# Reordering the beginning, the small pieces and the hand-over of an attention, gated attention and routing kernel

## The reference, cut to what matters

```python
# 1. token attention: convolutions of 3 taps, 8 heads of 16
q, k, v = (elu(conv3(x, W) + b) for W, b in ((WQ, BQ), (WK, BK), (WV, BV)))   # 8 x 748 x 128
h = softmax(q @ k.T / sqrt(16)) @ v
# 2. gated attention on layernorm(h): one more layernorm, expand, gelu gate, causal softmax
#    with a position bias, project; added to h
# 3. routed feed-forward on layernorm(h): top 2 of 64 experts with shared weights, capacity 128,
#    gelu(x w1 + b1) w2 + b2, weighed by the router; added to h
```

## Time and profile before

| | us |
|---|---|
| median of 3 runs (lowest, highest) | 840.41 (840.29, 840.66) |
| the profiled execution | 839.29 |
| its span, first to last instruction | 837.5 |
| TensorE busy | 785.9 (94%) |
| VectorE busy | 680.9 (81%) |
| ScalarE busy | 511.1 (61%) |
| POOL busy | 270.5 (32%) |

### The profile page before, as it was taken

The page is one execution under the profiler, slowest core; times in us unless marked ns, Lnnn a source line. Parts: engine busy times, 40 slices in busy tenths (PEclk is TensorE's granted clock), DMA queues, the critical chain, the costliest instruction groups (busy, mean ns, idle before and its releaser), DMA issues. The chain is left out here.

```text
span 837.5 us, 15609 instructions
## 1 busy us (share of the span) xinstructions
PE 785.9 (94%) x5555; PEld 472.6 (56%) x5555; DVE 680.9 (81%) x1624; ACT 511.1 (61%) x1096; POOL 270.5 (32%) x281
## 2 busy tenths in 40 slices
PE   9699999999999999999999997758999999999997
PEld 5254554554554554554453432236698787887885
DVE  4898888899899899889889896437888787887866
ACT  4176776786786786786786766414646546456343
POOL 3572250252252251251352022413152333332312
PEclk9999999999999999999999999868999999999999
DMA  5370151161151162142133103000000000000001
GB/s 115 67 120 14 11 118 25 12 119 25 11 110 35 11 106 38 11 104 40 11 89 36 12 2 65 7 9 1 1 1 20 19 2 19 20 2 20 18 3 37
DMA packets 85676, 31.08 MB, mean 37 GB/s; under 512 B 58496, under 2 KB 84320, under 8 KB 85600
## 3 DMA queue, kind: packets, MB, share of 16 engines
q1 hardware_dynamic: 85360, 29.80, 19.7%
q10 hardware_dynamic: 240, 0.30, 0.2%
HBM read 4.76 MB, written 3.06 MB: 9 GB/s over the span
## 5 line engine op out<-in xcount | busy, mean ns | idle before, releaser
L446 ACT ACTIVATE probs<-ps_a 128x384 f32<-128x384 f32 (+1 forms) x732 | 304.3, 482 | 93.9 <-PE ps_a L640 85.3
L531 DVE TENSOR_REDUCE neg_max<-ps_a 128x1 f32<-128x512 f32 (+1 forms) x384 | 251.7, 679 | 42.1 <-PE ps_a L656 40.6
L640 PE MATMUL ps_a<-q_rep,k_rep 98*128 98x384 bf16 (+3 forms) x768 | 217.0, 326 | 4.5 <-DVE neg_max L533 1.6
L656 PE MATMUL ps_a<-k_rep,q_rep 96*128 96x512 bf16 (+3 forms) x768 | 202.9, 322 | 8.2 <-DVE neg_max L531 4.1
L671 PE MATMUL ps_pv<-probs,v_hat 128*32 128x364 f32 (+3 forms) x1536 | 141.9, 487 | 0.0
L640 PEld LDWEIGHTS ps_a<-q_rep,k_rep 98*128 98x128 bf16 (+1 forms) x768 | 77.9, 102 | 101.1 <-issue 37.8
L533 DVE TENSOR_REDUCE neg_max<-ps_a 128x2 f32<-128x472 f32 x192 | 122.2, 636 | 0.0
L656 PEld LDWEIGHTS ps_a<-k_rep,q_rep 96*128 96x128 bf16 (+1 forms) x768 | 77.6, 105 | 72.4 <-DVE neg_max L531 21.0
L671 PEld LDWEIGHTS ps_pv<-probs,v_hat 128*32 128x32 f32 (+1 forms) x1536 | 40.3, 109 | 55.2 <-issue 37.7
L296 POOL TENSOR_TENSOR out_n<-out_r,inv_sum 128x192 f32<-128x192 f32 x32 | 16.4, 513 | 116.3 <-DVE inv_sum L512 110.6
L270 POOL TENSOR_SCALAR qk_e<-qk_e 128x748 f32<-128x748 f32 x14 | 38.0, 2716 | 38.5 <-ACT qk_e L363 38.5
(11 more groups left out here) (225 smaller groups left out, 1171.4 us busy)
## 6 DMA issues: line engine op xcount, KB each, us to landing
q_rep<-parts_q SPq DMA_DIRECT2D x96, 96.0 KB, 3.7
k_rep<-parts_k SPq DMA_DIRECT2D x93, 96.0 KB, 3.8
hall<-out_n SPq DMA_DIRECT2D x256, 12.0 KB, 1.8
xT<-in_x SPq DMA_DIRECT2D x8, 375.0 KB, 4.1
out_h<-y_out SPq DMA_DIRECT2D x7, 320.0 KB
q_rep<-max_T SPq DMA_DIRECT2D x32, 6.0 KB
w_sb<-in_w_T SPq DMA_DIRECT2D x2, 256.0 KB, 3.5
out_h<-y_out SPq DMA_DIRECT2D x8, 54.0 KB
```

What stands on the lines that cost most here:

```text
L446: act.activation(probs[0:rows(kt), n % RING, 0:w], ps_a[0:rows(kt), 3 + n % 3, 0:w], ACT.Exp, scale=DH ** -0.5).then_inc(p_ready, 1)
L531: dve.tensor_reduce(neg_max[0:rows(t), 0, col:col + 1], ps_a[0:rows(t), c, :], AX.X, ALU.max, negate=True).then_inc(sc_max, 1)
L640: pe.matmul(out[0:rows(kt), 0:QW[qh]], k_rep[0:KM, cb % 2, h, kt * P:kt * P + rows(kt)], q_rep[0:KM, cb % 2, qh, h, 0:QW[qh]], start=True, ...
L656: last = pe.matmul(out, q_rep[0:KS, it % 2, t // QT, h, t % QT * P:t % QT * P + rows(t)], k_rep[0:KS, it % 2, h, 512:L] if c == 2 else k_r ...
```

## The change

- **Hand-over.** `spread(B - 1, 1)`, the last 16 DMAs of SP in the first block, goes to SP's program of the second block, behind the rows of unit 0's maxima there. `out_n` and its semaphore live longer for it. The statistics and scales of unit 7 go from iteration 0 to iteration 2 of the second block. `load` goes from the end of SP's unit 7 to its beginning, between the rows of the fourth quarter of unit 6 and `spread(6, 0)`.
- **Beginning.** The four pieces are now keys 0, keys 1, queries 0, queries 1, split at column 384 instead of 374, so that the first product needs only three pieces. w_k is loaded by ScalarE's queue, x first by SP. SP issues all twelve copies (six of keys, then six of queries); ScalarE issues none. The 2-row memset of `k_rep` goes ahead of POOL's other work.
- **Unit 0's small pieces.** The two copies of unit 1's keys go from VectorE to ScalarE (`first_copy_k`). `elu_v` goes from steps 2 and 4 to 9 and 10, `elu_qk` from (4, 0) and (10, 0) to (9, 2) and (11, 1), and on ScalarE `high_part` and `middle_part` of the queries go to (9, 3) and (11, 1), of the keys to (12, 1) and (14, 0).
- **Places in all other units** move by a fraction of a step or one step. POOL's order in a unit was: negative q, residue q, outputs of quarter 2, third part q, negative k, residue k, outputs of quarter 3, third part k, negative v0, negative v1. It becomes: negative q, outputs of quarter 2, residue q, negative k, third part q, outputs of quarter 3, residue k, negative v0, third part k, negative v1.

```diff
@@ SP, beginning
+        load_x(0)
+        sp.dma_start(b_col["k"][:, :], bk.rearrange("(c o) -> c o", o=1)).then_inc(loaded["k"], 16)
         load_w("q", wq)
-        load_x(0)
...
+        for t, j in sorted(enumerate(K_PART), key=lambda tj: tj[1]):
+            sp.wait_ge((p_hi, p_mid, p_split)[j], 2)
+            replicate_k(sp, 0, 0, t)
         for t, j in sorted(enumerate(Q_PART), key=lambda tj: tj[1]):
-            sp.wait_ge((p_hi, p_mid, p_split)[j], 2)
+            sp.wait_ge((p_hi, p_mid, p_split)[j], 3)
             replicate_q(sp, 0, 0, t)
...
@@ SP, units
                 maxima_rows(it - 1, 3)
-                spread(it - 1, 0)
+            if it == B - 1:
+                ahead["load"](sp)
+            if it > 0:
+                spread(sp, it - 1, 0)
...
-            if it == B - 1:
-                ahead["load"](sp)
         maxima_rows(B - 1, 3)
-        for g in range(NG):
-            spread(B - 1, g)
+        spread(sp, B - 1, 0)
@@ ScalarE, after_exp
-                if at == (2, 1):
+                if at == (2, 0):
                     exp_qk(n, "q")
-                if at == (4, 2):
+                if at == ((6, 0) if it > 0 else (9, 3)):
                     high_part(n, "q")
+                if it == 0 and at in ((3, 0), (5, 3)):
+                    first_copy_k(s // 5)
-                if at == (7, 3):
+                if at == (7, 0):
                     exp_qk(n, "k")
-                if at == (7, 3):
+                if at == ((8, 1) if it > 0 else (11, 1)):
                     middle_part(n, "q")
-                if at == (10, 0):
+                if at == ((10, 0) if it > 0 else (12, 1)):
                     high_part(n, "k")
-                if at == (12, 0):
+                if at == ((12, 0) if it > 0 else (14, 0)):
                     middle_part(n, "k")
@@ VectorE, between
-                if at in ((3, 1), (6, 0)):
+                if it > 0 and at in ((3, 1), (6, 1)):
                     copy_qk(n, 2 + (s - 3) // 3)
-                if at == (4, 0):
+                if it > 0 and at == (4, 1):
                     elu_qk(n, "q")
-                if at == (10, 0):
+                if it > 0 and at == (9, 1):
                     elu_qk(n, "k")
-                if at in ((18, 2), (22, 1)):
-                    elu_v(n, ((18, 2), (22, 1)).index(at))
+                if at in ((19, 0), (21, 0)):
+                    elu_v(n, ((19, 0), (21, 0)).index(at))
-            if at in ((6, 0), (12, 0), (18, 2)):
+            if at in ((6, 1), (12, 0), (18, 1)):
                 maxima(it, s // 6 - 1)
-            if at in ((17, 0), (23, 1), (5, 2), (11, 1)):
+            if at in ((17, 0), (23, 0), (4, 2), (11, 0)):
...
+            if it == 0 and at in ((9, 0), (10, 0)):
+                elu_v(0, s - 9)
+            if it == 0 and at in ((9, 2), (11, 1)):
+                elu_qk(n, "qk"[(s - 9) // 2])
@@ second block
+            if it == 0:
+                spread(sp, B - 1, 1)
-            if it == 0:
+            if it == 2:
                 G["scales"](pool, B - 1, plain_wait)
-            if it == 0:
+            if it == 2:
                 for done in spread_done:
-                    dve.wait_ge(done, 16 * GH * (P // 32) * B)
+                    dve.wait_ge(done, SPREAD * B)
                 G["statistics"](dve, B - 1, plain_wait)
```

More of the change, by code:

```diff
@@ L50, in plain_wait, with token_attention @@
     eng.wait_ge(sem, value)
-def token_attention(nc, ctx, hall, spread_done, ahead, x, wq, wk, wv, bq, bk, bv):
+def token_attention(nc, ctx, outputs_of, ahead, x, wq, wk, wv, bq, bk, bv):
+    hall, out_n, o_done, spread_done, spread = outputs_of
     def sb(name, shape, dt):
@@ L304, in _ @@
             n = it + 1
[L305 to L308 removed]
+            if n < B:
+                negative(n, "q")
+            if it == 0:
+                negative(n, "k")
+            else:
+                weigh_outputs(it - 1, 2)
+            if n < B:
+                residue(n, "q")
                 if it > 0:
[L310 to L312 removed]
+                    negative(n, "k")
+                third_part(n, "q")
+            if it > 0:
+                weigh_outputs(it - 1, 3)
             if n < B:
+                residue(n, "k")
+                negative(n, "v0")
+                third_part(n, "k")
                 if it == 0:
                     ones_rows(1)
[L316 removed]
                 negative(n, "v1")
@@ L1113, with gated_units @@
 AT = places()
-def gated_units(nc, ctx, G, hall, spread_done, out):
+def gated_units(nc, ctx, G, outputs_of, out):
+    hall, _, _, spread_done, spread = outputs_of
     def sb(name, shape, dt):
```

133 lines of the change are left out of this document (67 added, 66 removed).

## The result

| | before | after |
|---|---|---|
| median of 4 runs (lowest, highest), us | 840.35 (840.12, 840.66) | 833.25 (831.16, 834.34) |
| the profiled execution, us | 839.29 | 834.34 |
| its span, us | 837.55 | 832.61 |
| mean granted TensorE clock | 0.981 | 0.984 |

The ratio is 0.9912, 95% interval 0.9891 to 0.9934: faster by 0.9%. The forecast was 822.0 us with a range of 814 to 829. It was 11 us too low; the time lies above the range.

What follows compares the result with a forecast made beforehand. TensorE bounds a middle unit, VectorE unit 0's first steps. Terms -10.3 - 6.2 + 0.5 - 1.3 + 0.4 + 1.3 - 2.8 = -18.4 took 839.29 to 820.9, or 822.0 us at the median's level; range 814 to 829.

Steps and rivals of the forecast that it cites:

- The hand-over and the load: Change of blocks: sixteen DMA issues leaving SP's end gain 10.3 us, loading the second block's weights earlier gains 6.2.
- the load's +0.5: End of the first block: the load, now in front of spread(6, 0), costs 0.5 us, ends 0 and 2.5.
- its forecast case: Likeliest case, 822.0 us, chance 0.53: in unit 0, tile 24 waits 4.3 us for rows behind SP's twelve copies.
- the last starts at 19.4. It lands 3.5 us later: Beginning: SP's last of twelve copies lands so that the first product runs at about 23.1 instead of 24.26, -1.2 us.
- 0, if a landing of 4.1 and a crowded queue eat it: Beginning: the bound at which the -1.2 us term gains nothing; the other end was -2.8.
- Tile 24 waits from 55.7 to 60.0: Unit 0: TensorE, ready at 55.7, stands until quarter 1's rows arrive behind the copies of unit 1's queries.
- a new stall of 4.3: Unit 0: the cost in us of TensorE's wait at tile 24, set against 2.4 gained by beginning and pieces.
- +0.3 at quarter 0, behind a copy and a reduction: Every unit but unit 0: quarter 0's maxima come later, costing 0.3 us within a net -0.4 a unit, -2.8 in seven.
- Twelve small VectorE operations ... +0.4: Second block, iteration 2: unit 7's statistics, 1.8 us of VectorE, delay TensorE by 0.4 us, range 0 to 1.
- The clock's term: Start of the second block: a shorter pause leaves less time at half clock, -1.3 us, ends 0 and -3.
- one pause of this size only: Clock at the new block: the trace before has only one TensorE pause like that of 3.28 us, followed by half clock.
- the places cost: Rival for the units: ScalarE standing at the keys' middle part costs TensorE 0.5 us each, +3.5 for -2.8, 828.3 us; chance 0.12.

Runs made afterwards that it cites:

- e5: Changed kernel with ScalarE issuing the three copies of the keys' high part and SP the other nine: 834.82 us, ratio to the kernel before 0.9951.
- e13: Changed kernel with rows early in unit 0, quarter 0's maxima ahead, scales in iteration 3, and first queries' copies halved before the first product: 813.11 us.
- e14: Changed kernel with unit 0's queries' ELU, high, middle and third parts back at their old steps: 824.54 us, ratio to the kernel before 0.9815.
- e12: Changed kernel with 24 idle TensorE products in the stall at tile 24 of unit 0: 830.94 us, ratio to the kernel before 0.9907.
- e16: Changed kernel with ScalarE's high part of the queries at (5, 2) instead of (6, 0) in units 1 to 6: 824.18 us.
- e3: Changed kernel with the keys' second-half copy and quarter 0's maxima back ahead of reduction (6, 0) in units 1 to 7: 824.88 us.
- e4: Changed kernel with POOL computing unit 7's scales in iteration 3 of the second block instead of iteration 2: 831.98 us.
- e10: Kernel before with spread(7, 1) in the second block and unit 7's statistics and scales in iteration 2, load left in place: 828.91 us.
- e2: Changed kernel with SP sending quarter 1's rows ahead of the twelve copies of unit 1's queries in unit 0: 827.66 us.
- e15: Changed kernel with the edits of e14, e3 and e4 together: 813.83 us, ratio to the kernel before 0.9698.
- e7: Kernel before with the hand-over edits, new places in units 1 to 7 (quarter 0's maxima as in e3) and e4's scales; old beginning and unit 0: 815.44 us.
- e11: Kernel before with only the load of the second block's weights moved ahead of spread(6, 0): 834.07 us, ratio 0.9953.
- e9: Changed kernel with rows early in unit 0, e3's and e4's edits, and twelve idle TensorE products ahead of the first score product: 816.58 us.

## Why the prediction was wrong

**Right.** The hand-over and the load, term by term (10.8 for 10.3, 6.7 for 6.2), and that they add up, the load's +0.5 apart; `repeat_weights` behind the maxima; the second block's start. Right in kind: TensorE waits at tile 24 for rows that stand behind the copies, as its forecast case had it; quarter 2's wait is gone.

**The beginning: -1.2 predicted, +0.7 measured.** The step that failed is "the last starts at 19.4. It lands 3.5 us later". The 3.5 is the median of the queries' copies alone. The last of the twelve landed 4.6 us behind its issue, because the copies themselves and not the issues set the pace (e5, e13). The same could be read before, from the keys' copies, up to 45 us:
```profile
DMA to landing us min/median/max: 3.2/3.5/5.2
```
The 5.2 is the last of the twelve there too. My bound "0, if a landing of 4.1 and a crowded queue eat it" was the case. Another 0.5 us is scatter: the first copy went at 12.91 and not at 12.41, 4.3 us behind the first exponential in both (8.64 and 8.14 us). The convolution's first products took 0.85 to 0.97 us each up to 7.36, and before up to 6.30, and about 0.48 behind that, with the granted clock at 1.00 in both; over all profiles the first exponential lies between 7.3 and 8.6 us, with the old beginning as with the new.
The Trainium skill (DMA: Bandwidth & Descriptors, "Issuing engines are not separate DMA queues") has both halves, shared engines and saved issue time. The saved issue time, for which the prediction gave 1.9 us, didn't bring e5's first product forward; that two queues share the same engines agrees with e5, where copies landed up to 7.1 us behind their issue.

**Unit 0: +2.5 predicted, +8.5 measured.** "Tile 24 waits from 55.7 to 60.0" became 60.1 to 65.6. Ready late by 4.4: 1.65 of the first product, 1.6 of step 1 at half clock (3.39 us for 1.76), 1.0 of quarter 1's L527 (52.23 to 53.35, the end of POOL's third part). Released late by 5.6: middle part 50.83 for 47.7 and 3.0 of that reach SP, twelve copies 8.62 for 7.64, rows landing in 3.6 for 2.03 us behind the copies' data. So the stall itself is only 1.2 longer than the 4.3 predicted. With the 1.6 and the 1.0 ahead of it and 2.8 behind it these are 6.6 us, and the unit was 6.0 longer than forecast (the 1.0 shows in e14, where L527 met nothing and step 11 took 3.22 us for 4.17). The failed step is the stall's price, "a new stall of 4.3": the sum left out that TensorE's clock was at half behind it, 2.8 us (e12), although had shown it for a pause of 3.28: I counted the clock at the one place and not at the other. The same goes for the pause ahead of the first product, which stayed and was followed by half clock this time, the 1.6 us of step 1.

**Places: -2.8 predicted (-2.3 with the load's +0.5), +2.2 measured.** Units 1 to 6 took 2.9 us more, unit 7 0.7 less. "+0.3 at quarter 0, behind a copy and a reduction" was the failed step. The price was 1.2 us a unit, and nearly all of it VectorE held by POOL (e16). Without it the places are worth 0.96 a middle unit (e3), more than twice the 0.4 predicted. The earlier trace rows showed where POOL's instructions lie, and I used them for who waits for whose data only.
The Trainium skill has the rule that the prediction left out: SBUF — State Buffer, "Who interferes with whom", says that a VectorE operation with two SBUF inputs and a GpSimd operation that reads SBUF exclude each other, and the later one stands until the other is through. The traces agree to 0.03 us where L527 met a POOL operation of 128x748 or 128x192. Where it ran beside POOL's `TENSOR_TENSOR` of 128x6 (L1003, 1.36 us), in quarter 3 of units 6 and 7, it kept its 0.16 and 0.17 us, and so it did in the kernel before beside a POOL `TENSOR_SCALAR` of 128x748 (66.47, POOL's from 65.19 to 67.28), where the `CAST` right behind it took 0.65 us for 0.17 and ended with POOL's. So not every such pair stands, and why these don't stays open.

**Second block: -0.9 predicted, +1.1 measured.** "Twelve small VectorE operations ... +0.4" was right for VectorE and left out that the same edit moves eight operations of POOL, 5.5 us, ahead of `second_norm`: 1.15 more (e4). The clock's term was -0.6 and not -1.3, and it varies from run to run: in its first 20 us the second block was at half clock for 9.9 us and not for 13.0, in two stretches, of which the prediction had seen the first only. Up to the first product on `vals` and `p_T` it took 20.88 us for 21.44. Over the profiles of kernels that are the same there, this length goes with the time at half clock: 17.9 us with 3.4 (e14), 21.0 with 10.1 (e10), 21.4 with 12.9 (e12). The prediction's "one pause of this size only" passed over TensorE's 2.79 us ahead of the first product, behind which the clock was at full.

The rival "the places cost" (828.3) had the right sign for the wrong reason: ScalarE didn't stand at the keys' middle part.

## What to carry to other kernels

When a small operation moves in time, look at what runs on the engines that share its way to memory at the new place, not only at who waits for its result: 0.16 us became 1.55 here, six times over. Price a predicted stall of TensorE twice, once for the standing and once for the clock behind it. And for data that goes out in many DMAs take the landing time from the last one of a group as large, not from the median.

## What the runs showed of the hardware

- VectorE's `TENSOR_TENSOR` of 128x12 took 1.55, 1.12, 0.61 and 0.45 us when a POOL `TENSOR_TENSOR` of 128x748 or 128x192 ran, and ended each time within 0.03 us of it; without one 0.16, and 0.16 to 0.17 beside POOL's `TENSOR_TENSOR` of 128x6 or, once, its `TENSOR_SCALAR` of 128x748. VectorE's `TENSOR_SCALAR` from PSUM beside the operation of 128x748 kept its 0.60.
- The same pause of 2.8 to 2.9 us ahead of the first product was followed by half clock (1.2 GHz) in eight of ten profiles of kernels with the new beginning and by full clock (2.4 GHz) in two (e2, e15); a pause of 2.6 to 2.8 with the old beginning in two of five (e7, e11). With 0.46 us (e13) or 0.21 (e9) it was full behind the first product. The stall of 5.5 us at tile 24 was followed by half clock, and with idle products in its place by full clock (e12).
- Twelve copies of 96 KB between SBUF partitions needed 11.8 to 11.9 us from the first issue to the product that waits for all when SP issued them all, and 11.6 to 11.9 in the old order with three from ScalarE's queue; 12.5 in e5; nine's worth of bytes 9.5. Issued 0.65 us apart, they landed 0.78 us apart.
